# A gated two-layer transformer block on one core: constant rows copied within DRAM, gate products per half of the tokens, expert bias inside the product, and all expert low parts on VectorE

## The chip, the cores and the metric

The kernel runs on one core of a Trainium2 chip. The time is the device time of one launch in microseconds (us); three runs of the kernel before took 837.93 to 839.80 us, median 838.51. All durations of instructions come from one further, profiled execution.

The engines are named as in the profile: PE (TensorE, matmuls and transposes; PEld its weight loads), DVE (VectorE), ACT (ScalarE), POOL (GpSimd), and SP (SyncE), which here only issues DMAs; SPq is its queue.

## What is computed

Input are 1024 tokens (8 blocks of 128) of width 512 and a context of the same shape. In short:

```
h   = x + tanh(g)   * grouped_query_attention(norm(x), ctx)     # 32 query heads, 8 KV heads, 128 x 128 per block
h   = h + tanh(g')  * unperm(up/gelu/down of 16 small heads(perm(norm(h))))
h   = h + tanh(g)   * group_norm(Wz * (att * (Wt * ctx))) + ... # second layer's cross attention
l   = norm(h) @ gate_w.T + gate_b ;  e = argmax(l)              # 8 experts, one per token
out = h + tanh(g')  * (norm(h) @ expert_w[e].T + expert_b[e])
```

The reference is float32. The kernel gets that precision out of faster matmuls: a weight or activation is split into a high part (rounded to float32r) and a low part (the rest), and a product is the sum of three matmuls, high x high, low x high and high x low. ACT writes high parts (`..._hi`), another engine subtracts to make low parts (`..._lo`).

## The kernel before

There are four stages. `project_kv` makes keys and values and writes them to DRAM. `attention` runs 64 units (8 groups g of heads, 8 token blocks b). `middle` does the small-head layer and the second cross attention. `experts` routes the tokens and multiplies them. Each engine has its own instruction list, in the order in which the code writes it; semaphores are the only ties. An instruction that waits holds back all that stand behind it on its engine.

**Attention.** Its units are software-pipelined: a list of stages with an offset each, run by `run(eng, stages)`. Groups 0 and 7 are written out, groups 1 to 6 are a hardware loop over pairs of groups (`Fori`, three passes, so two jumps back). The first ACT instructions are the high parts of the first output weights (L604), of the first values (L611) and the statistics of the first queries (L618, `q_stats`). The queries of units 0 and 1 have one PSUM bank each; PE cannot go further until unit 0 is normalised by ACT, POOL and DVE and transposed (L828).

SP issues, per group, one load of query weights (L532), one of output weights (L534), halves of v (L523) and kT (L528), and then `fill(g)` (L542): it writes 2064 KB of constants (zeros, and a huge number in the four last columns) into one expert's region of the DRAM array `sorted_x`. There are eight fills, one per expert. Their source is one SBUF tile of 128 rows (`empty`, set by L724 and L725) read eight times. All of these are on one DMA queue.

**Routing.** `experts` first forms the rows (L1520, `xrow`): six blocks on DVE, two (`BY_POOL`) by ACT and POOL (L1419, L1458). PE transposes each block (L1685), ACT copies it (L1408), and PE multiplies it with the gate weights: for each block four products with the 128 x 128 tokens as weights and 8 columns moving (L1691). `choose(c)` finds the experts for half c of the blocks, `ranks(c)` and `position(c)` the row of each token in `sorted_x`, and POOL scatters the rows by indirect DMA (L1470). `rstd(c)` on POOL gives the scale that `choose(c)` needs (`xrstd_done`). SP waits for all eight scatters, then loads one tile of 128 rows after the other (L1392).

**Tiles.** There are 15 tiles: the first of each expert (t = 0 to 7) and seven whose expert is known only at run time. `run` interleaves: PE transposes tile t+1 (L1728) and multiplies tile t (L1750 to L1752, 12 matmuls). Low parts of expert weights are made by POOL for expert 0 of the order and for the fourth quarter (`LO_POOL`) of the rest (L1477), by DVE for the other three (L1617). The bias is scaled once by POOL (L1489, 128 x 4096) and added to each tile by POOL (L1497). DVE adds the product (L1665), POOL stores by indirect DMA (L1502).

Of the kernel before, what the change touches and what calls it, by code (L numbers as in the profile page):

```python
# [20 lines left out]
F32 = mybir.dt.float32  # L21
F32R = mybir.dt.float32r
# [7 lines left out]
B = 8  # L30
# [19 lines left out]
GATE_LOADS = 8  # L50
# [374 lines left out]
def attention(nc, d, s, block):  # L425


    with ExitStack() as ctx:
# [89 lines left out]
        def _(sp):  # L518
# [33 lines left out]
            for dst, src in ((s.gate_w[:, :, :], d.gate_w), (s.gate_b[:, :], d.gate_b), (s.eid[:, :], d.eid),  # L552
                             (s.rows_before[:, :], d.rows_before), (s.upto[:, :, :], d.upto), (s.base[:, :], d.base),
                             (s.extra_row[:, :], d.extra_row), (s.token[:, :], d.token)):
                sp.dma_start(dst, src).then_inc(s.gate_ld, 16)
            sp.wait_ge(q_done, 8 * G - 8)
# [5 lines left out]
        def _(act):  # L562
            act.wait_ge(qeps_set, 1)

# [68 lines left out]
            def copy_xT(u, b, g, odd):  # L633
                if after(u, b, g, HB - 1):
                    act.wait_ge(s.filled, 16 * E)
# [86 lines left out]
        def _(dve):  # L722
            dve.memset(qeps[:, :], P * EPS).then_inc(qeps_set, 1)
            dve.memset(s.empty[:, 0:D], 0.0).then_inc(s.empty_set, 1)  # L724
            dve.memset(s.empty[:, D:ROW], NOWHERE).then_inc(s.empty_set, 1)  # L725
            dve.memset(s.ones[:, :], 1.0).then_inc(s.ones_set, 1)
            for k in range(EXTRA):
                dve.memset(s.steps[:, k:k + 1], float(P * (k + 1))).then_inc(s.ones_set, 1)
            dve.wait_ge(mT_done, 1)
            dve.tensor_copy(s.mT[:, :], oT_ps[:, 0:P]).then_inc(mT_copied, 1)  # L730

# [50 lines left out]
            def copy_xT(u, b, g, odd):  # L782
                if after(u, b, g, HB - 1):
                    dve.wait_ge(s.filled, 16 * E)
# [118 lines left out]
def middle(nc, d, s, block):  # L903


    with ExitStack() as ctx:
# [66 lines left out]
        def _(sp):  # L973
# [19 lines left out]
            sp.wait_ge(res_done, B)  # L993
            sp.dma_start(s.exp_b[:, :, :], d.exp_b).then_inc(s.exp_b_ld, 16)
# [130 lines left out]
        def _(dve):  # L1125
# [54 lines left out]
            dve.scalar_tensor_tensor(out=s.gate_c[:, :, :], in0=sm_ps[:, 320:320 + E].unsqueeze(1).to_broadcast([P, KT, E]),  # L1180
# [41 lines left out]
        def _(pe):  # L1222
# [73 lines left out]
            pe.wait_ge(s.ones_set, 1)  # L1296
            for kt in range(KT):
                pe.matmul(sm_ps[:, 320:320 + E], s.ones[:, :], s.gate_w[:, kt, :], start=(kt == 0), stop=(kt == KT - 1))
# [21 lines left out]
def experts(nc, d, s, block):  # L1320
# [4 lines left out]
    with ExitStack() as ctx:  # L1325
# [13 lines left out]
        x3T = s.xn  # L1339
# [3 lines left out]
        scaled_z, x3_pool = m.sem("scaled_z"), m.sem("x3_pool_done")  # L1343
# [10 lines left out]
        w_hi_done, w_lo_done = m.sem("ew_hi_done"), [m.sem("ew_lo_dve_done"), m.sem("ew_lo_pool_done")]  # L1354
        bias_scaled, biased = m.sem("bias_scaled"), m.sem("biased")
# [556 lines left out]
```

## Time and profile before

| | |
|---|---|
| median of 3 runs | 838.51 us (837.93 to 839.80) |
| profiled execution | 846.05 us, its span 844.3 us |
| mean granted PE clock | 0.945 of full speed |
| PE busy | 766.3 us (91% of the span) |
| DVE, ACT, POOL busy | 479.6, 481.6, 354.3 us |
| DMA | 89.78 MB, mean 106 GB/s |

Busy shares are averages over stages. The chain that ended last is 67% PE, 7% DVE, 5% ACT, 4% "issue", 2% DMA: most of the time PE sets the pace, and the rest lies in a few places where PE waits for another engine. A row of the timeline gives the start in us from the span's start, the duration, the engine, the line and operation, and in brackets the idle time before it and what ended it; "issue" there means that no semaphore explains the wait.

### The profile page before, as it was taken

The page shows a single profiled execution, that of the slowest core. Times are in us where ns is not written, and L with a number is a line of the kernel's source. Part 1 is how long each engine was busy: PE and PEld are TensorE (multiplying, and loading weights), DVE is VectorE, ACT ScalarE, POOL GpSimd, SP SyncE. Part 2 cuts the span into 40 slices and gives each one's busy share as a digit, 9 for nine tenths or more (in the row PEclk, how much of TensorE's full clock was granted, in tenths as well). Part 3 has the DMA queues.
Part 4 walks back from the last instruction along what each step waited for, and adds up shares of the span by engine and source line. Part 5 has one row for each costly group of instructions (what it writes and reads, how often), then busy time and mean ns, then how long its engine had stood idle before and what let it go on. Part 6 is the DMA issues. An engine that isn't in the chain of part 4 may idle for free.

```text
span 844.3 us, 13599 instructions
## 1 busy us (share of the span) xinstructions
PE 766.3 (91%) x3916; PEld 617.0 (73%) x3916; DVE 479.6 (57%) x876; ACT 481.6 (57%) x1815; POOL 354.3 (42%) x652
## 2 busy tenths in 40 slices
PE   5999988999999997999997999999999788583787
PEld 3888867888888876888886888888886334482665
DVE  4775315556556545565563565655666457743973
ACT  5543247766766755766664667677564464623542
POOL 0330034533534442444352354353233355639666
PEclk9999999999999998999998999999999799755899
DMA  8535562050050050015015005003200546713122
GB/s 306 179 121 157 184 199 76 14 211 28 14 205 30 11 195 37 13 50 187 13 31 195 25 12 212 25 13 120 100 2 1 184 164 226 324 38 138 40 87 87
DMA packets 49881, 89.78 MB, mean 106 GB/s; under 512 B 5407, under 2 KB 25887, under 8 KB 46240
## 3 DMA queue, kind: packets, MB, share of 16 engines
q1 hardware_dynamic: 46640, 80.73, 28.1%
q0 software_dynamic: 3184, 8.41, 2.8%
q8 instruction: 21, 0.34, 0.2%
q14 instruction: 36, 0.29, 0.1%
HBM read 55.42 MB, written 35.54 MB: 108 GB/s over the span
## 4 chain that ended last, share of the span: by engine, by line
PE 67%; DVE 7%; ACT 5%; issue 4%; DMA 2%; POOL 1%; POOLq 0%; ACTq 0%; SPq 0%; DVEq 0%
PE banks L849 7%; PE banks L850 7%; PE banks L851 7%; PE banks L819 6%; PE banks L821 6%; PE banks L820 6%; PE banks L809 6%; PE banks L828 3%; PE banks L836 3%; DVE ew_lo L1617 2%; PE banks L861 2%; PE banks L860 2%; PE banks L862 2%; PE banks L1274 2%; PE banks L1691 1%
## 5 line engine op out<-in xcount | busy, mean ns | idle before, releaser
L573 ACT ACTIVATE p_sb<-p_sb,nmax 128x128 f32<-128x128 f32 x256 | 99.7, 391 | 131.8 <-DVE nmax L743 131.8
L666 POOL TENSOR_TENSOR v_lo<-v_raw,v_hi 128x128 fp32r<-128x128 f32 x64 | 29.5, 461 | 271.5 <-ACT v_hi L611 271.5
L766 DVE TENSOR_TENSOR pT_lo<-banks,pT_hi 128x512 fp32r<-128x512 f32 x64 | 44.2, 691 | 51.0 <-ACT pT_hi L586 51.0
L809 PEld LDWEIGHTS banks<-kT,qT_sb 128*128 128x128 f32 x512 | 66.8, 191 | 7.2 <-ACT qT_sb L581 1.9
L734 DVE TENSOR_TENSOR oT_lo<-banks,oT_hi 128x512 fp32r<-128x512 f32 x64 | 44.1, 689 | 44.8 <-ACT oT_hi L568 44.8
L671 POOL TENSOR_TENSOR p_sb<-p_sb,rsum 128x512 f32<-128x512 f32 x64 | 66.5, 1039 | 5.6 <-DVE rsum L762 5.6
L809 PE MATMUL banks<-kT,qT_sb 128*128 128x128 f32 x512 | 67.6, 275 | 1.4 <-ACT qT_sb L581 1.4
L618 ACT ACTIVATE q_junk<-banks 128x128 f32<-128x128 f32 x256 | 66.1, 273 | 1.8 <-PE banks L821 1.8
L568 ACT ACTIVATE oT_hi<-banks 128x512 fp32r<-128x512 f32 x64 | 38.2, 596 | 47.3 <-PE banks L862 34.9
L772 DVE SCALAR_TENSOR_TENSOR x_sb<-banks,tgates,x_sb 128x512 f32<-128x512 f32 x64 | 48.0, 751 | 23.6 <-PE banks L851 23.6
L398 PE MATMUL banks<-w_hi,ctx_hi 128*128 128x512 f32 x128 | 53.8, 420 | 8.1 <-DVE ctx_lo L329 8.0
L849 PE MATMUL banks<-w_hi,oT_hi 128*128 128x512 f32 x128 | 54.4, 425 | 0.0
L750 DVE TENSOR_SCALAR q_val<-q_ss 128x4 f32<-128x4 f32 x64 | 31.7, 495 | 40.0 <-ACT q_junk L618 40.0
L849 PE MATMUL banks<-odd_hi,oT_hi 128*128 128x512 f32 x128 | 53.4, 417 | 0.4 <-DVE oT_lo L734 0.2
L819 PE MATMUL banks<-odd_hi,xT_hi 128*128 128x512 f32 x128 | 53.0, 414 | 0.0
L618 ACT ACTIVATION_READ_ACCUMULATOR q_junk<-banks 128x1 f32 x256 | 53.0, 207 | 0.0
L819 PE MATMUL banks<-w_hi,xT_hi 128*128 128x512 f32 x128 | 52.9, 414 | 0.0
L762 DVE RECIPROCAL rsum<-prob_sum 128x4 f32<-128x4 f32 x64 | 11.4, 178 | 72.0 <-ACT p_sb L573 72.0
L828 PE MATMUL banks<-ident_sb,q_sb 128*128 128x128 f32 x256 | 39.7, 278 | 13.7 <-DVE q_sb L756 13.6
L850 PE MATMUL banks<-w_hi,oT_lo 128*128 128x512 f32 x128 | 51.5, 402 | 0.0
L851 PE MATMUL banks<-w_lo,oT_hi 128*128 128x512 f32 x128 | 51.3, 401 | 0.0
L400 PE MATMUL banks<-w_lo,ctx_hi 128*128 128x512 f32 x128 | 51.1, 399 | 0.0
(265 smaller groups left out, 2190.2 us busy)
## 6 DMA issues: line engine op xcount, KB each, us to landing
sorted_x<-empty SPq DMA_DIRECT2D x8, 2064.0 KB, 8.8
w_raw<-in_wq_l SPq DMA_DIRECT2D x8, 1024.0 KB, 10.8
w_raw<-in_wo_l SPq DMA_DIRECT2D x8, 1024.0 KB, 6.3
exp_w<-in_exp_w_l SPq DMA_DIRECT2D x8, 1024.0 KB, 8.5
kT_scr<-kT_st SPq DMA_DIRECT2D x16, 256.0 KB
v_scr<-v_st SPq DMA_DIRECT2D x16, 256.0 KB, 2.3
xs<-sorted_x SPq DMA_DIRECT2D x15, 258.0 KB, 2.9
v_raw<-v_scr SPq DMA_DIRECT2D x14, 256.0 KB, 2.6
```

Of the source, the lines that this page charges most:

```text
L398: pe.matmul(kv_ps[i % 3][:, :], ctx_hi[:, kt, tok], hi, start=(kt == 0), stop=False)
L400: last = pe.matmul(kv_ps[i % 3][:, :], ctx_hi[:, kt, tok], lo, start=False, stop=(kt == KT - 1))
L573: last = act.activation(p_sb[:, b % 2, h * P:(h + 1) * P], p_sb[:, b % 2, h * P:(h + 1) * P], ACT.Exp, bias=nmax[:, b % 2, h:h + 1], accum ...
L618: last = act.activation(junk[:, h * P:(h + 1) * P], q_ps[b % 2][:, h * P:(h + 1) * P], ACT.Square, accum_out=ss[:, b % 2, h:h + 1])
L671: pool.tensor_tensor(blocks(p_sb[:, b % 2, :]), blocks(p_sb[:, b % 2, :]), per_block(rsum[:, b % 2, :], P), ALU.mult).then_inc(p_done, 1)
L809: last = pe.matmul(s_ps[:, h * P:(h + 1) * P], qT_sb[:, b % 2, h * P:(h + 1) * P], kT[:, b * P:(b + 1) * P], start=True, stop=True)
L819: pe.matmul(q_ps[b % 2][:, :], xh, wq_hi[odd][:, kt, :], start=(kt == 0), stop=False)
L820: pe.matmul(q_ps[b % 2][:, :], xl, wq_hi[odd][:, kt, :], start=False, stop=False)
L828: last = pe.transpose(qT_ps[:, h * P:(h + 1) * P], q_sb[:, b % 2, h * P:(h + 1) * P], s.ident[:, :])
L849: pe.matmul(o_ps[b % 2][:, :], oh, wo_hi[odd][:, h, :], start=(h == 0), stop=False)
L850: pe.matmul(o_ps[b % 2][:, :], ol, wo_hi[odd][:, h, :], start=False, stop=False)
L851: last = pe.matmul(o_ps[b % 2][:, :], oh, wo_lo[odd][:, h, :], start=False, stop=(h == HG - 1))
```

## The change

Five edits, all in one step:

1. A fill copies from a constant array in DRAM (`in_empty`) into `sorted_x`, both contiguous. The SBUF tile and its two memsets go. The wait of `copy_xT` for the fills becomes a wait for the stored bias; POOL's wait for all fills ahead of the scatter stays.
2. The expert bias (8 x 512) is loaded in front of attention, split into high and low part by ACT and DVE, stored to DRAM as two rows, and loaded again in `experts`. It enters each tile's product as one more matmul, with two rows of ones as weights. `add_bias`, the scaling and the 2048 KB load go.
3. The gate product runs per half: four matmuls of 32 gate columns against 512 tokens, each into its own 32 partitions, one ACT copy, and four small matmuls with a matrix `fold` that sums the four parts.
4. DVE forms all eight row blocks. All low parts of expert weights are on DVE; those of the first four experts are made before the first tile. POOL keeps `rstd`, scatters and stores.
5. `ranks(1)` adds the first half's counts with one matmul in place of four.

```diff
             def fill(e):
-                sp.dma_start(d.sorted_x[e].rearrange("(k p) n -> p k n", p=P),
-                             s.empty[:, :].unsqueeze(1).to_broadcast([P, B, ROW])).then_inc(s.filled, 16)
+                sp.dma_start(d.sorted_x[e].rearrange("(p k) n -> p (k n)", p=P), d.empty).then_inc(s.filled, 16)
...
-            sp.wait_ge(s.empty_set, 2)
             fill(0)
+            sp.dma_start(s.exp_b[:, :], d.exp_b).then_inc(s.exp_b_ld, 16)
             loads(1)
...
+            sp.wait_ge(s.exp_b_split, 2)
+            sp.dma_start(d.exp_b2[0], s.exp_b_hi[:, :].bitcast(F32)).then_inc(s.exp_b_stored, 16)
+            sp.dma_start(d.exp_b2[1], s.exp_b_lo[:, :].bitcast(F32)).then_inc(s.exp_b_stored, 16)
...
         @block.scalar
         def _(act):
             act.wait_ge(qeps_set, 1)
+            act.wait_ge(s.exp_b_ld, 16)
+            act.activation(s.exp_b_hi[:, :], s.exp_b[:, :], ACT.Copy).then_inc(s.exp_b_split, 1)
...
             act.wait_ge(s.recycled, 1)
-            act.wait_ge(s.a_done, 1)
-            for b in BY_POOL:
-                act.activation(s.z[:, b, :], s.z[:, b, :], ACT.Identity, scale=s.a_col[:, b:b + 1]).then_inc(scaled_z, 1)
-            split_w(0)
...
+            copy_gateT(1)
+            for n in range(READY):
+                split_w(n)
...
-            run([(split_x, 1), (normalise, 2), (split_next_w, 2)])
+            run([(split_x, 1), (normalise, 2), (split_next_w, 3)])
...
         @block.gpsimd
...
-            split_w(0, (0, 1))
             rstd(0)
-            split_w(0, (2, 3))
-            rstd(1)
             pool.wait_ge(s.filled, 16 * E)
             pool.wait_ge(s.token_set, 2)
             scatter(0)
-            pool.wait_ge(s.exp_b_ld, 16)
+            rstd(1)
             scatter(1)
-            pool.tensor_scalar(s.exp_b[:, :, :], s.exp_b[:, :, :], s.tgates[:, 3:4], None, ALU.mult).then_inc(bias_scaled, 1)
...
-            run([(split_next_w, 1), (add_bias, 0), (store, -1)])
+            for t in range(TILES):
+                store(t)
...
         @block.vector
...
             position(1)
+            list_tiles()
+            for n in range(READY):
+                split_w(n)
...
-            run([(split_x, 1), (add_y, -1), (split_next_w, 1)])
+            run([(split_x, 1), (add_y, -1), (split_next_w, 2)])
...
         @block.tensor
...
-            def gates(b):
-                pe.wait_ge(x3T_copied, b + 1)
+            def gates(c):
+                pe.wait_ge(x3T_copied, HB * (c + 1))
                 for kt in range(KT):
-                    last = pe.matmul(logit_ps[b // HB][:, b % HB * E:(b % HB + 1) * E], x3T[:, b % 2, kt * P:(kt + 1) * P],
-                                     s.gate_c[:, kt, :], start=(kt == 0), stop=(kt == KT - 1))
+                    last = pe.matmul(gateT_ps[c][32 * kt:32 * kt + 32, :], s.gate_c[:, kt, :], x3T[c][:, kt, :],
+                                     start=True, stop=True)
+                last.then_inc(gateT_done, 1)
+
+            def logits(c):
+                pe.wait_ge(gateT_copied, c + 1)
+                for b in range(HB):
+                    last = pe.matmul(logit_ps[c][:, b * E:(b + 1) * E], gateT[:, c, b * P:(b + 1) * P], s.fold[:, :],
+                                     start=True, stop=True)
                 last.then_inc(logit_done, 1)
...
+                if t == 0:
+                    pe.wait_ge(exp_b_ld, 16)
+                pe.matmul(out, s.ones_r[:, :], s.exp_b2[:, e, :], start=True, stop=False)
```

On SP, at the start of attention, in the difference from before to after (`exp_b` is the bias tile, `in_empty` the constant array):

```order
-L542 DMA sorted_x<-empty 128x8x516
+L542 DMA sorted_x<-in_empty 48x11008
+L547 DMA exp_b<-in_exp_b 8x512
```

The bias load stands right behind the first fill, which has become 48 runs of 11008 elements. On ACT, at the same place, before:

```order
L561 UNCONDITIONAL_BRANCH
L604 ACTIVATE w_hi_52<-w_raw_54 128x512 x2
L611 ACTIVATE v_hi<-v_raw 128x128
L618 ACTIVATE q_junk,q_ss<-banks0 128x128 x4
L622 ACTIVATE q_lnss<-q_ss,qeps 128x4
L624 ACTIVATE q_seed<-q_lnss 128x4
```

and after:

```order
L563 UNCONDITIONAL_BRANCH
L567 ACTIVATE exp_b_hi_66<-exp_b_65 8x512
L608 ACTIVATE w_hi_52<-w_raw_54 128x512 x2
L615 ACTIVATE v_hi<-v_raw 128x128
L622 ACTIVATE q_junk,q_ss<-banks0 128x128 x4
L626 ACTIVATE q_lnss<-q_ss,qeps 128x4
```

The first instruction of ACT in attention is now one that reads the bias, ahead of the weights and the statistics. On POOL, in routing, before (`xrow` in the fourth of each group of small operations is the scale of one half):

```order
L1477 TENSOR_TENSOR ew_lo<-exp_w,ew_hi 128x512 x2
L75 TENSOR_TENSOR xtmp<-xseed 128x4
L77 TENSOR_TENSOR xtmp<-xtmp,xval 128x4
L79 TENSOR_TENSOR xtmp<-three_halves,xtmp 128x4
L81 TENSOR_TENSOR xrow<-xseed,xtmp 128x4
L1470 DMA sorted_x<-xrow,pos_i 8192x516 x8
L1489 TENSOR_SCALAR exp_b<-exp_b,tgates 128x4096
```

and after:

```order
L81 TENSOR_TENSOR xrow<-xseed,xtmp 128x4
L1468 DMA sorted_x<-xrow,pos_i 8192x516 x4
L75 TENSOR_TENSOR xtmp<-xseed 128x4
L77 TENSOR_TENSOR xtmp<-xtmp,xval 128x4
L79 TENSOR_TENSOR xtmp<-three_halves,xtmp 128x4
L81 TENSOR_TENSOR xrow<-xseed,xtmp 128x4
L1468 DMA sorted_x<-xrow,pos_i 8192x516 x4
```

The second half's scale has moved behind the first four scatters, and POOL's tensor work around them is gone.

## Rows read from the trace of the kernel before

**Rows 1.** Timeline at the start of attention
```profile
114.31 1.15 ACT L604 ACTIVATE w_hi<-w_raw 128x512 fp32r<-128x512 f32 x2 [1.80 <-DVE qeps L723]
114.96 0.37 SPq L542 DMA_DIRECT2D sorted_x<-empty  x1
...
117.45 0.28 ACT L618 ACTIVATE q_junk<-banks 128x128 f32<-128x128 f32 x1 [1.79 <-PE banks L821]
...
121.12 0.66 PE L828 MATMUL banks<-ident_sb,q_sb 128*128 128x128 f32 x4 [0.99 <-DVE q_sb L756]
```
**Rows 2.** Timeline of SP's queue at the last fill
```profile
577.76 0.41 SPq L542 DMA_DIRECT2D sorted_x<-empty  x1
578.38 0.41 SPq L555 DMA_DIRECT2D gate_w<-in_gate_w_l  x1
```
**Rows 3.** The instructions of the tile gate_w
```profile
DMA to landing us min/median/max: 7.5/7.5/7.5
```
**Rows 4.** DMA issues: count, size each, median us from issue to landing
```profile
sorted_x<-empty SPq DMA_DIRECT2D x8, 2064.0 KB, 8.8
...
kT<-kT_scr SPq DMA_DIRECT2D x14, 256.0 KB, 2.9
```
**Rows 5.** A stretch of middle: busy us of PE, PEld, DVE, ACT, POOL, then PEclk, DMA share, GB/s
```profile
720.00:729.70 9.70, 2.38 (x7) 1.01 (x7) 6.70 (x24) 7.57 (x14) 6.36 (x9) 0.91 1.03 435
```
**Rows 6.** Timeline of ACT at the first of the two jumps back of attention's loop
```profile
317.72 0.60 ACT L568 ACTIVATE oT_hi<-banks 128x512 fp32r<-128x512 f32 x1 [6.08 <-issue]
```
**Rows 7.** Timeline of SP's queue in attention
```profile
304.68 0.33 SPq L528 DMA_DIRECT2D kT<-kT_scr  x1
...
306.14 0.34 SPq L532 DMA_DIRECT2D w_raw<-in_wq_l  x1
...
376.50 0.33 SPq L528 DMA_DIRECT2D kT<-kT_scr  x1
...
440.71 0.33 SPq L528 DMA_DIRECT2D kT<-kT_scr  x1
```
**Rows 8.** The instructions of line L532
```profile
DMA to landing us min/median/max: 10.0/11.0/11.3
```
**Rows 9.** The stretch of routing, in the columns of rows 5
```profile
728.80:770.00 41.20, 26.39 (x124) 25.83 (x124) 18.03 (x51) 10.63 (x22) 22.70 (x23) 0.50 0.29 113
```
**Rows 10.** Timeline of POOL and DVE in routing
```profile
748.94 0.20 POOL L75 TENSOR_TENSOR xtmp<-xseed 128x4 f32<-128x4 f32 x1 [6.32 <-ACT xseed L1403]
...
754.56 1.04 POOL L1470 DMA_INDIRECT sorted_x<-xrow,pos_i  x1 [4.58 <-DVE pos_i L1576]
...
755.04 0.19 DVE L1560 TENSOR_TENSOR hot<-cand,first 128x32 f32<-128x32 f32 x1
...
759.57 0.17 DVE L1576 CAST pos_i<-pos 128x4 int32<-128x4 f32 x1
...
760.55 0.96 POOL L1470 DMA_INDIRECT sorted_x<-xrow,pos_i  x1 [1.14 <-issue]
```
**Rows 11.** Groups by line from 690 us: busy us, mean ns, idle before and releaser
```profile
L1691 PE MATMUL banks<-gate_c,xn 128*128 128x8 f32 x64 | 13.9, 348 | 1.2 <-ACT xn L1408 1.2
...
L1665 DVE SCALAR_TENSOR_TENSOR xs<-banks,tgates,xs 128x512 f32<-128x512 f32 x15 | 11.1, 741 | 3.3 <-PE banks L1752 3.3
```
**Rows 12.** Timeline of PE in middle, products of 32 columns of weights
```profile
673.24 1.94 PE L1284 MATMUL banks<-hid,down 128*32 128x512 f32 x8
```
**Rows 13.** Timeline of the tiles
```profile
774.27 0.78 PE L1750 MATMUL banks<-ew_hi,xsT_hi 128*128 128x512 f32 x1
...
785.00 1.88 DVE L1617 TENSOR_TENSOR ew_lo<-exp_w,ew_hi 128x512 fp32r<-128x512 f32 x3
...
799.64 5.71 DVE L1617 TENSOR_TENSOR ew_lo<-exp_w,ew_hi 128x512 fp32r<-128x512 f32 x3
...
816.09 0.60 PE L1728 MATMUL banks<-ident_sb,xn 128*128 128x128 f32 x4
...
832.14 0.66 PE L1728 MATMUL banks<-ident_sb,xn 128*128 128x128 f32 x4
```

More of the change, by code:

```diff
@@ L723, in _ @@
             dve.memset(qeps[:, :], P * EPS).then_inc(qeps_set, 1)
-            dve.memset(s.empty[:, 0:D], 0.0).then_inc(s.empty_set, 1)
-            dve.memset(s.empty[:, D:ROW], NOWHERE).then_inc(s.empty_set, 1)
             dve.memset(s.ones[:, :], 1.0).then_inc(s.ones_set, 1)
+            dve.memset(s.gate_c[:, :, :], 0.0).then_inc(s.ones_set, 1)
+            dve.wait_ge(s.ones_set, 2)
+            dve.tensor_copy(s.ones_r[:, :], s.ones[0:2, :]).then_inc(s.ones_set, 1)
             for k in range(EXTRA):
@@ L1295, in _ @@
             pe.wait_ge(s.gate_ld, 16 * GATE_LOADS)
-            pe.wait_ge(s.ones_set, 1)
+            pe.wait_ge(s.ones_set, 3)
             for kt in range(KT):
-                pe.matmul(sm_ps[:, 320:320 + E], s.ones[:, :], s.gate_w[:, kt, :], start=(kt == 0), stop=(kt == KT - 1))
+                pe.matmul(sm_ps[:, 320:320 + E], s.ones[:, :], s.gate_w[:, kt, 0:E], start=(kt == 0), stop=(kt == KT - 1))
             pe.matmul(sm_ps[:, 0:B], s.group_mean[:, :], s.zmv[:, :, 0], start=True, stop=True).then_inc(gmean_done, 1)
@@ L1406, in copy_x3T, with copy_gateT @@
                 act.wait_ge(x3T_done, b + 1)
-                reached(act, logit_done, b - 1)
-                act.activation(x3T[:, b % 2, :], x3T_ps[b % 2][:, :], ACT.Copy).then_inc(x3T_copied, 1)
+                act.activation(x3T[b // HB][:, :, b % HB * P:(b % HB + 1) * P], blocks(x3T_ps[b % 4][:, :]), ACT.Copy)\
+                    .then_inc(x3T_copied, 1)
+            def copy_gateT(c):
+                act.wait_ge(gateT_done, c + 1)
+                act.activation(gateT[:, c, :], gateT_ps[c][:, :], ACT.Copy).then_inc(gateT_copied, 1)
             def split_w(n):
@@ L1697, in _ @@
             pe.wait_ge(s.row_done, B)
-            for b in range(B):
+            for b in range(HB):
                 transpose_x3(b)
-                if b:
-                    gates(b - 1)
-            gates(B - 1)
+            gates(0)
+            transpose_x3(4)
+            transpose_x3(5)
+            logits(0)
+            transpose_x3(6)
+            transpose_x3(7)
+            gates(1)
+            logits(1)
             def ranks(c):
@@ L1712, in ranks @@
                 if c:
-                    for k in range(HB):
-                        last = pe.matmul(rank_ps[c][:, k * E:(k + 1) * E], s.ones[:, :], hot_sum[:, 0, :],
-                                         start=False, stop=(k == HB - 1))
+                    last = pe.matmul(rank_ps[c][:, cols(0)], s.ones[:, :], hot_sum[:, 0, :].unsqueeze(1).to_broadcast([P, HB, E]),
+                                     start=False, stop=True)
                 last.then_inc(rank_done, 1)
```

145 lines of the change are left out of this document (58 added, 87 removed).

## The prediction

> **What bounds the kernel now.** I read the page first: PE is busy 91% of the span, so attention, where PE runs without gaps, gives nothing back by itself, and only places where PE waits can move. Then the waits and the timeline at those places. Four stand out.
>
> (a) The start of attention. ACT begins at 114.31 and takes the first queries' statistics at 117.45; PE's transposes of that unit follow at 121.12, after a wait of 0.99 us [rows 1]. Here the chain ACT, POOL, DVE, PE sets the pace and not PE's work.
>
> (b) The two jumps back of the loop. ACT stands still 6.08 us at the first, with "issue" as the reason [rows 6]; the second is alike. The time between the kT loads that mark a group is 376.50 - 304.68 = 71.8 us with a jump in it and 440.71 - 376.50 = 64.2 us without [rows 7]: 7.6 us lost for 6.1 us of ACT standing still, the other 1.5 us being the half clock on which PE restarts. The jump falls into the time of a fill and of a weight load issued right behind it at 306.14 [rows 7]; the load lands 11.0 us later [rows 8], at 317.1, and ACT resumes at 317.72.
>
> (c) Routing: 41.2 us with PE busy 26.39 at clock 0.50, that is 1.2 GHz, throughout [rows 9]. The end is set by the second half: its scatters start at 760.55, 6.0 us behind the first half's [rows 10].
>
> (d) The first eight tiles: from PE's first product at 774.27 to the transposes ahead of the ninth product at 816.09 are 41.8 us for eight tiles, 5.2 each; then the transposes run from 816.09 to 832.14 in five steps, 3.21 us a tile [rows 13]. In the slow part three low parts take 1.88 us on DVE when POOL lets it, and 5.71 us when POOL works beside it [rows 13]: 0.63 and 1.9 us apiece.
>
> **The start of attention: a new wait.** ACT now waits for the bias, and the bias is issued behind a fill. What a small load behind a fill costs is in the trace: gate_w is issued 0.62 us after the last fill and lands 7.5 us later [rows 2, 3], so 8.1 us after the fill's issue. SP no longer waits for the memset and can issue with ACT's first at about 114.3. The bias lands at 122.4 if the copy is as fast as the fill now. Add 0.5 for the new activation (an estimate from the 0.6 us that 128 x 512 takes) and 1.4 for the weights and values ahead of the statistics (the 1.15 of rows 1 plus one small one): 124.3 in place of 117.45, or 7 us. Behind the waiting instruction stand all of ACT's; DVE, POOL and PE wait for them, and PE has only two query banks to fill meanwhile. Nothing hides it, and nothing later gives it back, since PE has no slack in the groups that follow. With the restart at half clock as in (b), 1.5 us more: **8.5 us**, at equal speed of the fill.
>
> The speed of a copy within DRAM is the unknown, X us more than now until landing. A fill of 2064 KB lands in 8.8 us, 256 KB in 2.9 [rows 4]; so some 2 us are fixed and the data takes 6.8. Lower end: the runs are 44 KB in place of 2 KB and move at the highest rate of any stretch, 435 GB/s [rows 5], 4.9 us, X = -1.9. If reads and writes together are held to 435 GB/s, 4.23 MB take 9.7 us, X = +2.9. Upper end: every byte costs twice, X = +6.8. I take X = +2, between the same speed and the shared 435, since writes at about 310 and reads at 435 both occur and each must now be served at once. The start then costs **10.5 us**.
>
> The Trainium skill speaks against this edit: "DMA: Bandwidth & Descriptors", section "Latency and other measured facts", gives about 207 to 214 GB/s per direction for copies between HBM tensors. By that figure, as an estimate, the copy's data takes 9.9 us, X would be +3.1 and the whole sum, with the jumps below, about 2 us higher than mine. No row of before shows such a copy.
>
> **The jumps back.** If ACT's resumption waits for the queue to empty, as 317.1 against 317.72 suggests, each jump costs X more; if it only falls together with it, nothing. Bounds 0 and X for each of two; I take half, **+2 us** in all.
>
> The Trainium skill, "Runtime: NRT & Kernel Launch", section "Instruction fetch mechanics", says that a taken branch out of the fetched window forces a fetch by DMA; the standstill without a semaphore at just two jumps [rows 6] agrees. "DMA: Bandwidth & Descriptors", "Queues, rings and completion order", says that the DMA engines change between queues packet by packet. By that rule the fill's duration would not matter but the length of its runs would, and 44 KB at 435/16 GB/s per engine is 1.6 us of waiting for one packet, nearly the same +2 to +3 us in all.
>
> The other fills hide as before: no instruction of ACT waits for a weight load in the trace. The two stores of the bias and the ninth small load stand behind the last fill, a whole group ahead of their reader.
>
> **Routing.** The gate products are 64 matmuls, 13.9 us busy on PE [rows 11], 0.22 apiece. The new ones have the form of L1284: four calls, eight matmuls, 1.94 us at half clock [rows 12]; twice that, and eight small products of two matmuls each (3.5), make 7.4. PE needs 6.5 us less; with the extra copy of 0.6 and a start that is bound by the row blocks, I let the first half's scatter start 4 us earlier, at 750.5. But the end is set by the second half. Its `rstd(1)` stood at 748.94, ahead of the first scatter at 754.56 [rows 10]. Now it is behind four scatters of 1.21 ((760.55 - 754.56 - 1.14)/4), and `shift(1)` and `choose(1)` on DVE, `ranks(1)` on PE, `position(1)` on DVE and the last four scatters, and behind them SP's first tile load, wait for it in a row. From the first scatter's start: scatters 4.9; scale, four operations of 0.2 and their gaps, 1.1; shift and choice, eight operations of 0.19 and their gaps, 1.8; from the choice (755.04) to the positions (759.57) 4.7 now, less three products of 0.43 in `ranks`, 3.4; hand-over to POOL 760.55 - 759.57 = 1.0. Together 12.2 us against 6.0 now. 750.5 + 12.2 = 762.7 against 760.55: tiles start **2 us later**. Bounds: 1 us earlier (the first half ready by 747.5) and 4 later (only by 752.5).
>
> **Tiles.** DVE makes 16 low parts after the tile list, 16 x 0.63 = 10 us, about as long as scatters, load and first transposes take; first product at 776.3. POOL has no tensor work left, so a low part stays at 0.63. Per tile DVE needs 0.74 for the sum [rows 11], 0.7 for the low part of the tokens (an estimate from the same size) and 4 x 0.63, 4.0 us in four tiles, PE 3.21 + 0.23 for the bias matmul = 3.44. The four tiles with ready weights let DVE run ahead, so PE sets the pace but for about 1 us. Product 0 at half clock is 5.5, a transpose group 0.5, seven tiles at 3.44 are 24.1, plus 1: 31.1 us against 41.8, **-10.7**. The last seven tiles take seven bias matmuls more, **+1.6**. Bounds for both together: -12 (no DVE delay) and -3 (low parts take (1.88 + 5.71)/6 = 1.27 us on DVE all the same).
>
> **Sum.** 10.5 + 2 + 2 - 10.7 + 1.6 = **+5.4 us**; I take +5. The profiled execution (846.05 around a span of 844.3) would go to 851, and the median of the runs shown, which is 7.5 us below it, from 838.5 to **843.5**.
>
> **Rivals.**
> *The copy is fast* (X = -1.9). For it: one long run per descriptor and 435 GB/s [rows 5]; against it: reading and writing the same memory at once. Start 6.6, jumps -1.9 to -3.8, routing and tiles -7.1: -2.4 to -4.3, so 834 to 836. This is the one that ends faster; it is told from no change below X = -1, since 8.5 - 7.1 = +1.4 remains at X = 0 and the jumps follow.
> *The copy is slow* (X = +4 to +6.8) and the jumps follow it fully: +1.4 + 3X, that is 852 to 860. For it: ACT resumes within 0.6 us of the weights' landing.
> *The tiles gain little*: DVE, alone with all low parts, becomes the bound, or the 16 early ones hold back the first tile: sum +8 to +13, 846.5 to 851.5. Against it: the 1.88 us in [rows 13].
> *The new wait isn't felt*, because the bias passes the fill on the queue: then 10.5 falls to 1 or 2 and the time is about 835. Against it: gate_w, which did not pass its fill [rows 3].
>
> **Chances.** Forecast 0.45 (839.5 to 847), fast copy 0.2, slow copy 0.15, little gain at the tiles 0.12, bias passes 0.08. A difference below 0.2% (1.7 us) cannot be told from none. Faster takes the fast copy and the passing bias but for a little at their edge, 0.26; the same is the low edge of the forecast and that little, 0.11; slower is the rest, 0.63. The range that leaves out 2 in 10 is 834 to 852; the forecast alone has 839.5 to 847.
>
> **What would show it.** In the profile after: ACT's first instruction in attention at 123 to 127 with a DMA named as what it waited for, and PE's first transposes of queries near 130; SP's kT loads with a jump between them 72 to 75 us apart, and without 64.2; POOL's `rstd(1)` behind four scatters and the fifth scatter 11 to 13 us behind the first; low parts on DVE near 0.63 us; tiles 3.4 to 3.5 us apart from the second on. I am wrong if the first transposes of attention come before 124 or the tiles stay above 4.5 us.

## The result, and the profile after

The changed kernel takes 844.39 us (843.19 to 845.42, 4 runs), the kernel before beside it 838.80 (837.93 to 839.80): a ratio of 1.0066 (1.0046 to 1.0085), +5.6 us where +5 was predicted, inside the range. Timed again later it is 1.0053 (1.0035 to 1.0071). The sum was right; several of its terms were not, and that is what the rest is about.

The profiled executions stand the other way round: 843.73 us now (span 841.9) against 846.05 (span 844.3). So I first cut both spans at the same seven points of the program. The last two columns of times are a second profile of each kernel, taken with the experiments on two different chips.

| stretch, us | before | changed | before, again | changed, again | predicted |
|---|---|---|---|---|---|
| to the first kT load of L528 | 144.2 | 154.2 | 144.0 | 156.5 | +10.5 |
| to its last kT load | 433.1 | 432.3 | 432.7 | 430.8 | +2 |
| to SP's first store of xT_scr | 81.1 | 81.0 | 81.0 | 81.0 | 0 |
| to POOL's yrstd, L81 (end of middle) | 70.1 | 64.8 | 68.8 | 64.6 | 0 |
| to the first scatter | 26.2 | 18.5 | 26.2 | 18.6 | -4 |
| to the tiles' first transposes | 16.4 | 22.5 | 16.4 | 22.7 | +6 |
| to the end of the span | 73.3 | 68.5 | 71.6 | 68.2 | -9.1 |

Leave out the fourth row, which is not the change's (below), and the first pair gives +2.9, the second +5.9 us, around the timed +5.6 and +4.5. On the page PE is busy 761.2 us (90%), DVE 470.9, ACT 481.3 and POOL 306.4, 48 less than before; 87.76 MB are moved; the chain is 79% PE and 4% DMA.

**Start of attention.** The timeline of the changed kernel; SPq is SP's queue, and the last row is from the page's DMA issues (count, size each, median us to landing):

```profile
114.36 0.61 SPq L542 DMA_DIRECT2D sorted_x<-in_empty  x1
115.03 0.53 SPq L547 DMA_DIRECT2D exp_b<-in_exp_b  x1
...
123.52 0.63 ACT L567 ACTIVATE exp_b_hi<-exp_b 8x512 fp32r<-8x512 f32 x1 [11.57 <-DMA exp_b<-in_exp_b]
124.05 1.13 ACT L608 ACTIVATE w_hi<-w_raw 128x512 fp32r<-128x512 f32 x2
...
129.41 1.11 PE L836 MATMUL banks<-ident_sb,q_sb 128*128 128x128 f32 x4 [8.28 <-DVE q_sb L764]
```
```profile
sorted_x<-in_empty SPq DMA_DIRECT2D x8, 2064.0 KB, 9.3
```

Against [rows 1] ACT's first instruction is at 123.52 in place of 114.31, behind 11.57 us that a DMA ended, though 16 KB were all it needed: they were issued 0.67 us behind 2 MB. PE waits 8.28 us in place of 0.99. The fill lands in 9.3 us and not 8.8 [rows 4]: the copy's X was +0.5.

**The jumps back.** ACT at the first jump, and SP's kT loads:

```profile
326.93 0.60 ACT L572 ACTIVATE oT_hi<-banks 128x512 fp32r<-128x512 f32 x1 [5.69 <-issue]
```
```profile
314.53 0.33 SPq L528 DMA_DIRECT2D kT<-kT_scr  x1
...
386.22 0.33 SPq L528 DMA_DIRECT2D kT<-kT_scr  x1
...
450.33 0.33 SPq L528 DMA_DIRECT2D kT<-kT_scr  x1
```

5.69 us for 6.08 [rows 6], and 71.7 and 64.1 us for 71.8 and 64.2 [rows 7]. The fill is only 0.5 us slower, so that alone is a weak test. The weight load at each jump tells more. This is the second jump in the kernel with the bias product over 128 rows (below), with the load's time from issue to landing:

```profile
453.29 0.35 SPq L532 DMA_DIRECT2D w_raw<-in_wq_l  x1
...
464.39 0.60 ACT L572 ACTIVATE oT_hi<-banks 128x512 fp32r<-128x512 f32 x1 [5.98 <-issue]
```
```profile
DMA to landing us min/median/max: 13.0/13.0/13.0
```

The load lands at 466.3, and ACT has gone on at 464.39. In the changed kernel too ACT resumes ahead of the landing, by 0.2 us at the first jump and 0.5 at the second. So the jump does not wait for that load. Over all profiles of this case ACT stands still 5.2 to 7.0 us at a jump, 5.5 to 6.3 where the fills come from SBUF.

**Routing and the first transposes of a tile:**

```profile
738.69 1.94 PE L1661 MATMUL banks<-x3T,gate_c 128*32 128x512 f32 x8 [0.69 <-ACT x3T L1412]
...
750.88 1.04 POOL L1468 DMA_INDIRECT sorted_x<-xrow,pos_i  x1 [10.43 <-DVE pos_i L1547]
...
755.77 0.22 POOL L75 TENSOR_TENSOR xtmp<-xseed 128x4 f32<-128x4 f32 x1
...
762.53 0.99 POOL L1468 DMA_INDIRECT sorted_x<-xrow,pos_i  x1 [5.70 <-DVE pos_i L1547]
...
773.35 1.11 PE L1709 MATMUL banks<-ident_sb,xn 128*128 128x128 f32 x4 [11.67 <-ACT xn L1442]
```

The wide product has the 1.94 us of [rows 12]. rstd(1) now stands at 755.77, behind four scatters, where [rows 10] had it ahead of the first, and the fifth scatter is 11.65 us behind the first, not 6.0.

**Tiles.** DVE's low parts ahead of them, then one tile on PE (the product before it left out):

```profile
763.98 9.71 DVE L1588 TENSOR_TENSOR ew_lo<-exp_w,ew_hi 128x512 fp32r<-128x512 f32 x16
...
805.94 0.60 PE L1709 MATMUL banks<-ident_sb,xn 128*128 128x128 f32 x4
806.46 0.18 PEld L1724 LDWEIGHTS banks<-exp_b,ones_r 2*128 2x128 f32 x1 [0.17 <-issue]
806.47 0.49 PE L1724 MATMUL banks<-exp_b,ones_r 2*128 2x512 f32 x1
806.88 0.19 PEld L1729 LDWEIGHTS banks<-ew_hi,xsT_hi 128*128 128x128 f32 x1 [0.24 <-issue]
806.88 0.50 PE L1729 MATMUL banks<-ew_hi,xsT_hi 128*128 128x512 f32 x1
807.22 0.40 PE L1730 MATMUL banks<-ew_hi,xsT_lo 128*128 128x512 f32 x1
...
809.79 0.60 PE L1709 MATMUL banks<-ident_sb,xn 128*128 128x128 f32 x4
```

A low part takes 0.61 us on DVE, where [rows 13] had up to 1.9. A tile takes 809.79 - 805.94 = 3.85 us, from the second to the last, where the prediction had 3.44. The extra is not in one row: products follow each other every 0.23 us, but from the transposes to the bias product it is 0.53, and from there to the next 0.41.

### The profile page after: what moved, and what is told of

It reads as the page before. It is cut to its first block, busy times and chain, and to the rows that moved or that the text cites. A ratio compares the mean times of both kernels' runs of the same rounds, so it can differ in the third digit from the quotient of the medians.

```text
span 841.9 us, 13494 instructions
## 1 busy us (share of the span) xinstructions
PE 761.2 (90%) x3893; PEld 605.5 (72%) x3893; DVE 470.9 (56%) x890; ACT 481.3 (57%) x1816; POOL 306.4 (36%) x623
## 2 busy tenths in 40 slices
DMA packets 42125, 87.76 MB, mean 104 GB/s; under 512 B 5561, under 2 KB 26041, under 8 KB 38226
## 4 chain that ended last, share of the span: by engine, by line
PE 79%; DVE 5%; ACT 4%; DMA 4%; issue 4%; POOL 2%; SPq 1%; POOLq 0%; ACTq 0%; DVEq 0%
PE banks L857 7%; PE banks L858 7%; PE banks L859 7%; PE banks L829 6%; PE banks L828 6%; PE banks L827 6%; PE banks L817 6%; PE banks L836 4%; PE banks L400 3%; PE banks L398 3%; PE banks L844 3%; PE banks L399 3%; PE banks L1729 2%; PE banks L1730 2%; PE banks L1731 2%
## 5 line engine op out<-in xcount | busy, mean ns | idle before, releaser
L817 PE MATMUL banks<-kT,qT_sb 128*128 128x128 f32 x512 | 68.5, 277 | 1.4 <-ACT qT_sb L585 1.4
L836 PEld LDWEIGHTS banks<-ident_sb,q_sb 128*128 128x128 f32 x256 | 31.8, 144 | 30.8 <-DVE q_sb L764 24.1
```

The source lines that it names most:

```text
L817: last = pe.matmul(s_ps[:, h * P:(h + 1) * P], qT_sb[:, b % 2, h * P:(h + 1) * P], kT[:, b * P:(b + 1) * P], start=True, stop=True)
L836: last = pe.transpose(qT_ps[:, h * P:(h + 1) * P], q_sb[:, b % 2, h * P:(h + 1) * P], s.ident[:, :])
```

## Experiments

Each set of four ran on one chip with its own runs of the kernel before, whose medians were 844.94, 840.95 and 845.30 us. So I compare ratios to it, and turn a difference into us with 840. The changed kernel was repeated in the second set only; a difference to it carries both intervals, some 2 us either way (3 for the last set).

| kernel | ratio to before (95%) |
|---|---|
| bias ahead of the fill | 0.9957 (0.9941 to 0.9973) |
| bias split later | 0.9942 (0.9922 to 0.9962) |
| before with the copy only | 1.0034 (1.0014 to 1.0053) |
| changed, again | 1.0053 (1.0035 to 1.0071) |
| rstd(1) early | 0.9971 (0.9958 to 0.9985) |
| bias over 128 rows | 0.9978 (0.9963 to 0.9993) |
| no bias | 0.9946 (0.9926 to 0.9966) |
| three mendings | 0.9792 (0.9753 to 0.9832) |
| the same, fills from SBUF | 0.9772 (0.9735 to 0.9809) |
| POOL's sum beside | 1.0089 (1.0058 to 1.0120) |
| before with the wait only | 1.0078 (1.0054 to 1.0102) |

### The start: is it the wait?

Bias issued ahead of the fill:

```diff
-            fill(0)
             sp.dma_start(s.exp_b[:, :], d.exp_b).then_inc(s.exp_b_ld, 16)
+            fill(0)
```

> The changed kernel with one thing altered: SP issues the 16 KB load of the biases ahead of fill 0 and not behind it. If the start is lost to the queue (the load stands behind 2 MB of fill), the load lands in at most the 2.9 us that 256 KB take, ACT's first instruction moves from 123.5 to 116.5 to 117.5 and the first transposes of queries from 129.4 to 122.5 to 123.5: 6 to 7 us less, about 838 us, level with the kernel before. If the copy from DRAM to DRAM is itself what slows the start (by the traffic beside it), or if what is lost at the start is given back later by some slack, the gain is under 2 us, 842.5 to 844.5.

Bias split inside the first group, the load behind the fill as in the changed kernel:

```diff
-            act.wait_ge(s.exp_b_ld, 16)
-            act.activation(s.exp_b_hi[:, :], s.exp_b[:, :], ACT.Copy).then_inc(s.exp_b_split, 1)
+            def bias_split(u, b, g, odd):
+                if isinstance(g, int) and g == 0 and b == 4:
+                    act.wait_ge(s.exp_b_ld, 16)
+                    act.activation(s.exp_b_hi[:, :], s.exp_b[:, :], ACT.Copy).then_inc(s.exp_b_split, 1)
```

(the low part likewise on DVE at b == 6; both are added to the lists that `run` gets)

> The changed kernel with nothing of the biases ahead of attention: the load stays behind fill 0, but ACT's high part and DVE's low part are made inside the first group (units 4 and 6), when the load has long landed. If the whole loss at the start is the wait, the first transposes come at 121.1 as in the kernel before, 8 us or 9 with the restart at half clock, and the time is 835 to 836, below the kernel before: routing and tiles together would then be worth about -3. If the wait is only a part of it, ACT starts at 114.3 but PE's first groups stay longer than before (64.1 us), and the time is 838 or more.

And the kernel before with the wait alone:

```diff
             fill(0)
+            sp.dma_start(s.probe[:, :], d.probe).then_inc(s.probe_ld, 16)
...
             act.wait_ge(qeps_set, 1)
+            act.wait_ge(s.probe_ld, 16)
```

> The kernel before with the new wait alone: a 16 KB load behind fill 0, and ACT waits for it before its first instruction; nothing uses it. By the prediction's term at an equal fill the start costs 8.5 us: ACT's first instruction at 122.5 to 123, 847 against 838.5. In the profiles with such a wait so far the stretch from xT_scr to yrstd is 4 us shorter (64.7 against 68.6 and more). If that goes with the wait, it shows here too, and the time rises by only 4 to 5; if it goes with the other parts of the change, the stretch stays at 68.6 and the time rises by 8 to 9.

The first rows of ACT in the three timelines, in that order:

```profile
117.04 0.63 ACT L567 ACTIVATE exp_b_hi<-exp_b 8x512 fp32r<-8x512 f32 x1 [4.07 <-DMA exp_b<-in_exp_b]
```
```profile
114.72 1.15 ACT L611 ACTIVATE w_hi<-w_raw 128x512 fp32r<-128x512 f32 x2 [1.77 <-DVE qeps L730]
```
```profile
123.89 1.15 ACT L606 ACTIVATE w_hi<-w_raw 128x512 fp32r<-128x512 f32 x2 [11.16 <-DMA probe<-in_exp_b]
```

Alone on the queue the same load is there at 117.04; behind the fill at 123.5 to 125.3 in every profile that waits. Taking the wait out of the changed kernel gives 1.0053 - 0.9942 = 0.0111, 9.3 us, and the load's place alone 8.1; both bring it below the kernel before. Put into the kernel before, the wait costs 0.0078, 6.6 us (4.5 to 8.6), where I had expected 8 to 9. The start is the wait, 7 to 9 us; the rival that slack gives all of it back is out. Some is made up: ACT starts 9.2 us late in the changed kernel and 9.6 in the kernel with the wait only, the first kT load is 10.1 and 10.3 us late, the last one, at the end of attention, 9.3 and 8.0 (586.55 and 585.26 for 577.24). With the place alone changed I had 6 to 7 and got 8.1, within the two intervals.

### The copy by itself

```diff
             def fill(e):
-                sp.dma_start(d.sorted_x[e].rearrange("(k p) n -> p k n", p=P),
-                             s.empty[:, :].unsqueeze(1).to_broadcast([P, B, ROW])).then_inc(s.filled, 16)
+                sp.dma_start(d.sorted_x[e].rearrange("(p k) n -> p (k n)", p=P), d.empty).then_inc(s.filled, 16)
```

> The kernel before with one thing altered: the sixteen fills read a constant tensor in DRAM (two long runs of 44 KB and less per descriptor) and not the tile in SBUF. Nothing waits for a fill but the scatters, so the start is as before. The prediction had each jump back of the loop follow the longer queue, +2 us in all: 840.5. What the changed kernel's trace suggests is that the jump does not care: groups of 71.7 to 72.3 us with a jump and 64.1 without, time 838.5 within 0.7. If the copy disturbs PE or the weights' landing over all 16 groups, it is more than +2.

(There are eight fills in eight groups, not sixteen.) It is +2.9 us (1.2 to 4.5), so my expectation of nothing was a miss. The jumps are a small part: ACT stands still 6.89 us at the first, and the kT loads around it are 380.52 - 307.79 = 72.7 us apart, 0.9 more than before; around the second it is 72.3, as before. Most of its loss in the profile is at the start. Windows of it and of the second profile of the kernel before; after the busy times come PE's granted clock, DMA share and GB/s:

```profile
110.00:120.00 10.00, 7.68 (x29) 6.03 (x28) 1.02 (x12) 2.80 (x12) 2.94 (x3) 0.83 0.56 194
120.00:130.00 10.00, 8.32 (x37) 6.56 (x35) 3.19 (x7) 5.85 (x27) 4.52 (x11) 0.83 0.58 184
```
```profile
110.00:120.00 10.00, 7.66 (x34) 5.74 (x32) 1.19 (x13) 4.11 (x15) 3.58 (x7) 1.00 0.62 219
120.00:130.00 10.00, 7.66 (x44) 6.26 (x45) 4.42 (x9) 6.83 (x33) 5.96 (x13) 1.00 0.69 232
```

PE was idle 2.32 us at 112 to 114 in both, and one came back at 1.2 GHz, the other at 2.4. But the same fall is in the kernel with the wait only, which fills from SBUF, and is not in the changed kernel's second profile, which copies. Of all the profiles, seven of the ten that copy have a fall between 114 and 118, and one of the four that fill from SBUF: the copy may make it likelier, but so few can't show it. The pair at the end of this section tries it again.

> The kernel before once more, for a second profile. Its first profiled execution took 846.05 us against a median of 838.8. If that was an accident of the one execution (PE at half clock and gaps between 691 and 702, some 5 us), this profile has a span of 837 to 840 and the stretch from 658 to 704 is 4 to 5 us shorter. If it belongs to the kernel, the span is 843 to 845 again and the unprofiled runs hide it.

That second profile of the kernel before came out at 842.85 us, span 840.8: 3.5 us below the first, but with 68.8 us in the middle, so the stretch was not an accident of one execution. The runs of the kernel before in this set spread over 841 to 849, and a run with more half clock tends to be longer: the span is on average 840.9 us at a mean clock of 0.951 (two runs), 842.3 at 0.947 (five, 839.8 to 844.5), 846.6 at 0.940 (one).

> The changed kernel once more, unaltered, timed on the same chip as the experiments on its parts, since the kernel before spreads from 841 to 849 there and lay at 838.8 on the first. Expected is the first ratio again, 1.0066 (1.0046 to 1.0085). If the start costs 9 and the two experiments on it gave it back, those ratios (0.9957 with the bias ahead of the fill, 0.9942 with nothing waiting) mean 1.003 to 1.007 here. Half clock for a few us at 113 to 116 is expected in its profile again if the kernel brings it, and not if it is chance.

1.0053, as expected; ACT's first instruction at 124.62. PE was at full clock at 114 this time and at half from 124 on. So the fall at 114 is not there in every execution of the kernel; the one during the long wait is in all seven profiles that have the wait (0.50 to 0.60 from 125 to 130).

### Routing: rstd(1) ahead of the scatters

```diff
             rstd(0)
+            rstd(1)
             pool.wait_ge(s.filled, 16 * E)
             pool.wait_ge(s.token_set, 2)
             scatter(0)
-            rstd(1)
             scatter(1)
```

> The changed kernel with POOL's rstd(1) ahead of the first half's scatters. The prediction had the move behind them put the end of routing 12.2 us behind the first scatter in place of 6.0. By that the fifth scatter now starts 5 to 6 us after the first (11.65 in the changed kernel), first transposes of the tiles at 767 to 768 in place of 773.4, and the time falls by 5 to 6 us: 838.5 to 839.5. The rival: DVE makes sixteen low parts (9.7 us) behind the tile list, and they or the choice of the second half, now ahead of the first half's positions, hold the first tile: gain 0 to 3.

```profile
748.97 0.20 POOL L75 TENSOR_TENSOR xtmp<-xseed 128x4 f32<-128x4 f32 x1 [6.01 <-ACT xseed L1408]
...
753.73 1.05 POOL L1468 DMA_INDIRECT sorted_x<-xrow,pos_i  x1 [3.73 <-DVE pos_i L1547]
...
758.94 0.97 POOL L1468 DMA_INDIRECT sorted_x<-xrow,pos_i  x1 [0.30 <-issue]
```

The fifth scatter follows the fourth with no wait, 5.21 us behind the first; from the first scatter to the first transposes it is 17.0 us for 22.5. The time falls by 0.0082, 6.9 us (5.0 to 8.8; 5 to 6 expected). DVE's sixteen low parts end at 769.6 and its next work starts at 772.51 behind a wait of 2.88: they do not hold the tile, and the rival is out.

### The bias product: why 3.85 us a tile?

```diff
-        s.ones_r = m.sb("ones_r", [2, P], F32R)
+        s.ones_r = m.sb("ones_r", [P, P], F32R)
...
-            s.exp_b2, s.xn = beside("exp_b2", [2, E, D], 0, F32R), ...
+            s.exp_b2, s.xn = beside("exp_b2", [P, E, D], 0, F32R), ...
```

> The changed kernel with the bias product over 128 rows in place of 2: ones_r has ones in two rows and zeros in 126, exp_b2 the biases in two rows and finite values in the others (one more load of 2 MB in the shadow of the scatters); the products are the same. If it is the two-row product that costs 0.66 us a tile (the transposes ahead of it run 0.53 and not 0.36, gaps of 0.17 and 0.24 with nothing awaited around it), a tile falls from 3.86 to 3.43 us and the time by 15 x 0.43 = 6 us. If any thirteenth product costs that, the tile stays at 3.8 or more and the time does not move.

```diff
-                pe.matmul(out, s.ones_r[:, :], s.exp_b2[:, e, :], start=True, stop=False)
...
-                    pe.matmul(out, xsT_hi[:, t % 2, cols], s.ew_hi[:, e, kt, :], start=False, stop=False)
+                    pe.matmul(out, xsT_hi[:, t % 2, cols], s.ew_hi[:, e, kt, :], start=(kt == 0), stop=False)
```

> The changed kernel without the bias product: the sum of the experts' bias is left out of the result. The tile falls to the 3.20 us of the kernel before and the time by 15 x 0.66 = 9.9 us; by the prediction's 0.23 a tile it would be 3.5 us. A time that falls by less than the tiles' steps say would mean that the last tiles' stores, not PE, set the end.

A tile on PE with the bias over 128 rows, the product's twelve matmuls cut:

```profile
799.77 0.60 PE L1713 MATMUL banks<-ident_sb,xn 128*128 128x128 f32 x4
800.12 0.48 PE L1728 MATMUL banks<-exp_b,ones_r 128*128 128x512 f32 x1
800.44 0.39 PE L1733 MATMUL banks<-ew_hi,xsT_hi 128*128 128x512 f32 x1
...
803.24 0.60 PE L1713 MATMUL banks<-ident_sb,xn 128*128 128x128 f32 x4
```

3.47 us a tile, and without the bias 3.23 (798.34 to 801.57). So a bias matmul costs 0.24 us over 128 rows and 0.62 over two; with 128 rows the stretch from the first transposes to the end is 61.3 us for 68.5. The times agree: 0.0075, 6.3 us, for the form (6 expected), and 0.0107, 9.0 us, for leaving it out (9.9 expected). The form cost more than the work. Without the bias the profiled execution does not show its gain in that stretch, 62.1 us: it was the slowest of the six (838.88 for a median of 836.13), and two of its tiles took 5.6 and 5.3 us in place of 3.23. Ahead of the first of them ACT waits 3.51 us for the load of a tile, which SP can issue only when an earlier tile is stored. The rival (any thirteenth product costs it) is out.

The Trainium skill, "TensorEngine Tiling (Array Packing)", section "Key Properties", says that changing the tiling mode drains TensorE. The row that it fits is the weight load of the two-row product, which comes 0.17 us late with "issue" as the reason, and the next one 0.24 us late; over 128 rows neither gap is there. No run here shows the drain itself, nor that the two-row product is another mode: which part of the engine takes the time stays open.

### POOL beside DVE

```diff
+            pool.wait_ge(scattered, 16 * B)
             for t in range(TILES):
-                store(t)
+                pool.wait_ge(xn_done, t + 1)
+                if t:
+                    pool.wait_ge(added, t)
+                pool.tensor_tensor(xrow[:, 0, 0:D], xrow[:, 1, 0:D], xrow[:, 2, 0:D], ALU.add).then_inc(added, 1)
+                if t:
+                    store(t - 1)
+            store(TILES - 1)
```

> The changed kernel with one sum of 128 x 512 added on POOL for each tile, as the kernel before had for the biases; its result is used by nobody. If DVE's work beside POOL is what made the first eight tiles 5.2 us each before, low parts and sums of DVE that meet it take 1.2 us and more in place of 0.61, the tiles with low parts (4 to 7) grow from 3.86 to 4.4 or more, and the time by 2 to 4 us; the tiles behind them, where DVE idles 2.5 us each, do not change. If POOL's other work (the scaling of 10.65 us, its low parts) was the cause, nothing moves: under 0.7 us.

DVE and POOL in its timeline:

```profile
800.96 4.03 DVE L1596 TENSOR_TENSOR ew_lo<-exp_w,ew_hi 128x512 fp32r<-128x512 f32 x4
804.91 0.68 DVE L1642 TENSOR_TENSOR xsT_lo<-banks,xsT_hi 128x512 fp32r<-128x512 f32 x1
```
```profile
803.12 1.30 POOL L1491 TENSOR_TENSOR xrow<-xrow 128x512 f32<-128x512 f32 x1
```

Four low parts take 4.03 us for 2.5, more by 1.5 than they do alone, while one sum of 1.30 runs on POOL: DVE all but stands still for it. On DVE the four tiles with low parts go to 5.2 us each (794.48, 799.70, 804.91, 810.11, 815.30 are the starts of xsT_lo). DVE had some lead, so on PE three tiles grow, to 4.17, 5.21 and 5.21 us, 3.0 us in all, and the later ones stay at 3.86. The time rises by 0.0036 against the changed kernel's repeat, 3.0 us; with both intervals that is between nothing and 6, so the trace carries this reading (72.1 us from the tiles' first transposes to the end for 68.2 and 68.5). The stores stand behind the sums here as well; they can't be the cause, since the time is lost in DVE's low parts. So POOL can slow DVE as far as the 1.9 us for a low part in [rows 13]. That a tile took 5.2 us there too [rows 13] is an average over steps of 3.2 to 7.7, with POOL making low parts besides, and proves nothing more. The Trainium skill, "SBUF — State Buffer", section "Who interferes with whom", says that a tensor_tensor of VectorE with both inputs in SBUF contends with GpSimd's reads for a shared port pair; ew_lo has both there, and the trace agrees, 4.03 against 2.5. xsT_lo, with one input in PSUM, keeps its 0.69 where a sum of POOL runs beside it (at 820.66 and 824.53).

### All three mended

The edits of the bias split, rstd(1) and the bias product together.

> The changed kernel with all three mendings together: the split of the biases inside the first group, rstd(1) ahead of the first half's scatters, and the bias product over 128 rows. Timed alone against the kernel before they gave 0.9942, 0.9971 and 0.9978, where the changed kernel had 1.0053; if they add up, this has 1.0053 - 0.0111 - 0.0082 - 0.0075 = 0.9785, 18 us below the kernel before. If the middle of the kernel takes 4 us more whenever nothing is waited for at the start (64.6 to 64.8 us from xT_scr to yrstd in the five profiles with that wait, 68.6 to 70.8 in the five without), it is already in the first of these and nothing more is lost. The rival: with an earlier routing DVE's sixteen low parts hold the first product, and one of the gains is halved: 0.982 or more.

830.05 us beside 845.30: 0.9792, where the parts added up to 0.9785. It beats both kernels. Tiles are 3.47 us on PE; DVE needs 3.67 while it makes low parts, but its lead lasts through the four tiles. The stretch from the first scatter to the first transposes is 16.7 us, to the end 63.3. The rival of the expectation, that the sixteen low parts hold the first product, lies inside the interval of the time, and the trace rules it out: they end at 766.7, and DVE then waits 2.58 us for ACT. Two tiles behind those with low parts take 4.5 and 4.4 us, and ACT waits 2.42 and 1.56 us for their loads: some 2 us now lie in the loads, the next place to look.

```diff
             def fill(e):
-                sp.dma_start(d.sorted_x[e].rearrange("(p k) n -> p (k n)", p=P), d.empty).then_inc(s.filled, 16)
+                sp.dma_start(d.sorted_x[e].rearrange("(k p) n -> p k n", p=P),
+                             s.empty[:, :].unsqueeze(1).to_broadcast([P, B, ROW])).then_inc(s.filled, 16)
```

> The last kernel with the fills from a tile in SBUF again, as the kernel before has them, and so with the copy from DRAM alone undone. The kernel before with the copy alone was 1.0034 (1.0014 to 1.0053), all of it, by its profile, a lower granted clock at the start of attention (0.71 to 0.74 where the kernel before had 1.00), though PE stood idle equally long there. If the copy brings that, this is 2 to 3 us faster than the kernel with the copy and its clock at 115 is 1.00; if it was chance, the two agree within 1.5 us, and half clock at 115 can come in either.

827.72 us: 0.0020 less, 1.7 us, with intervals of 0.004 on each side. It has the sign of the copy's +2.9 but cannot tell it from nothing; in its profile the clock was full up to 120 and at half for a while behind it (0.83 from 120 to 130). By the two pairs together the copy costs something between nothing and 4.5 us; how much and why stays open.

## Why the prediction was right, and where it was wrong

**Start, +10.5.** Right in mechanism, in size a little high. The bias landed 0.9 us earlier than X = +2 had it (ACT at 123.5, not 124.4), PE's transposes came 8.3 us later, and a longer stretch at half clock behind the wait made 10.1 us of it at the first kT load, 12.5 in the repeat. In time the wait is 6.6 to 9.3 us by the three experiments, where 8.5 + X with the X that was measured gives 9.0. Of the 10.1, 0.8 us is made up by the last kT load, 1.9 of the 12.5; the fall of the clock at 114 may be another part.

**X = +2.** Too high: 9.3 us for 8.8, X = +0.5; 2064 KB in 9.3 us, with 2 us fixed, are, as an estimate, about 290 GB/s each way. So the rival of the slow copy fell. The rival of the fast copy fell too; X was not below -1. The bias did not pass the fill. The figure of 207 to 214 GB/s that the Trainium skill gives in "DMA: Bandwidth & Descriptors", "Latency and other measured facts", for tiles of 128 rows of 16 KiB, is below what this copy reached, and the +3.1 from it was further off than my +2.

**Jumps, +2.** Wrong. Neither jump grew in the changed kernel (71.7 and 72.1 us for 71.8 and 72.3). That ACT resumed 0.6 us behind the weights' landing [rows 6, 8] was coincidence: in the changed kernel it resumes ahead of it, and in the profile above 1.9 us ahead.

**Routing, +2.** Half right. The second half's tail was 11.65 us by the trace and 12.2 in the forecast. The first half was mis-sized: the first scatter came 7.7 us nearer to the end of middle, not 4. I let PE's saving of 6.5 us count only in part, "a start that is bound by the row blocks", and did not subtract what ACT and POOL no longer do ahead of it (the split of a first expert, scaled z, sums, low parts). That this is the rest is a reading of the code; no run took the 7.7 us apart. So, from the end of middle, the tiles start 1.7 us earlier (1.3 in the second pair), not 2 later. The early rstd(1) shows what the move cost: 6.9 us in time, 5.5 to 5.7 in the trace.

**Tiles, -10.7 and +1.6.** The first eight went from 41.8 to 32.2 us (777.62 to 809.79), and 1.0 us was lost ahead of the first product; the last seven products cost 3.9 us more. Together -4.7 for -9.1. The step that failed is "PE 3.21 + 0.23 for the bias matmul": the 0.23 is right for a matmul over 128 rows and was taken for one over two, which costs 0.6 or more. Fifteen times 0.4 is 6 us, the 6.3 of the experiment. Some of it was hidden: product 0 and DVE's delay were put at 7.0 us together and took 5.2. The other half, POOL off DVE's back, held.

**Middle, 0.** Right, though the profiles look as if it gained 4 to 5 us. The stretch is 64.6 to 64.8 us in the changed kernel's first profile and all four of set 2, and 68.6 to 70.8 in the first of the kernel before and all eight of sets 1 and 3, among them five that are the changed kernel with a part altered. ACT's activations in it, in the second profile of the kernel before and of the changed kernel:

```profile
688.36 1.26 ACT L1047 ACTIVATE hid<-banks 128x512 f32<-128x512 f32 x2 [0.63 <-PE banks L1274]
690.65 0.60 ACT L1047 ACTIVATE hid<-banks 128x512 f32<-128x512 f32 x1 [1.03 <-PE banks L1274]
693.38 1.57 ACT L1047 ACTIVATE hid<-banks 128x512 f32<-128x512 f32 x3 [2.14 <-PE banks L1274]
```
```profile
698.62 2.30 ACT L1053 ACTIVATE hid<-banks 128x512 f32<-128x512 f32 x4 [0.38 <-PE banks L1281]
701.30 1.09 ACT L1053 ACTIVATE hid<-banks 128x512 f32<-128x512 f32 x2 [0.38 <-PE banks L1281]
```

The same six instructions get through in 6.6 us in the first and 3.8 in the second, waiting for PE. Behind them PE's granted clock is 0.77 from 695 to 700 us in the first and 1.00 in the second, which would be the rest. It goes with the set, not with the edit, and the kernel before is 4 us slower where it is seen (844.94 and 845.30 against 840.95). I had taken the wait at the start for its reason before the last set, and the kernel with only the wait (69.4) refuted that. What it is stays open; it also explains most of why the two profiled spans stood the wrong way round.

So +5 came out right in part by luck: two terms that were too high by 6.5 to 7 us together (jumps and routing, by the two pairs) met one that was too favourable by 4.4 to 5.7 (tiles). What is left between the pairs of profiles and the timed differences, 2.7 us less in the first and 1.4 more in the second, lies within the chance of single profiles. The mechanism that made the kernel slower, the wait, was the one I had named and sized.

## What to carry to other kernels

A small load that something waits for goes ahead of a large one on its queue, or its reader goes later: here the order of two lines was worth 8 us, and with two more small edits the change turned from 0.5% slower to 2% faster. Before an edit is judged, ask of each instruction that it moves who is queued behind it (rstd(1): 6.9 us), and price a matmul by its form, not by its columns. Cut two profiled executions into stages before comparing their spans: here the spans had the wrong sign.

## What the runs showed that I had not expected

- A matmul of 512 columns over two rows between matmuls over 128 rows costs 0.62 to 0.66 us; over 128 rows, 126 of them zeros in the weights, 0.24.
- After the same 2.3 us of idle PE came back at 1.2 GHz in some profiles and at 2.4 in others, of one and the same kernel (changed, 0.50 from 114 to 116 in the first profile, full clock there in the second).
- ACT stands still 5.2 to 7.0 us at each jump back of the loop, in every profile, whether the weight load beside it has landed or not.
- One stretch of middle is 4 us longer in two of the sets, each on its own chip, than in the third, in every kernel of the set.
- With the tiles at 3.5 us and less, PE begins to wait for the tile loads (2.03 us at one tile without the bias).
- DRAM to DRAM landed 2064 KB in 9.0 to 9.5 us (medians) in the ten profiles that copy, 8.7 to 8.8 from SBUF in the other four: the queue hardly sees the difference.
